# Attention output kept for two blocks: out-projection, norms and FFN spread over all eight units of the next block, tokens held in two tiles

## The chip, the core and the metric

The kernel runs on one core of a Trainium2 chip. The metric is the device time of one execution in microseconds; lower is better. All values are fp32; the queries and keys are split into a rounded part and a remainder (type fp32r) for the score matmuls.

## What is computed

Two sequences of 2048 tokens, 1024 channels, pass through one transformer block. 32 query heads of 32 channels share one key head and one value head.

```python
# x (2, 2048, 1024); wq, wo (1024, 1024); wk, wv (1024, 32); A (8, 16, 1024); B (8, 1024, 16); Wr (8, 1024)
n = layernorm(x)
q, k, v = (n @ wq).reshape(2, 2048, 32, 32), n @ wk, n @ wv
scores = einsum('bqhd,bkd->bhqk', q, k) / sqrt(32)
scores = where(causal, scores, -inf)
attn = einsum('bhqk,bkd->bqhd', softmax(scores), v).reshape(2, 2048, 1024) @ wo
x = x + layernorm(attn)
n = layernorm(x)
gate = 8 * softmax(n @ Wr.T + br)
low = einsum('bsd,hrd->bshr', n, A)
ffn = 2.0 * einsum('bshr,hor,bsh->bso', low, B, gate)
out = x + layernorm(ffn)
```

## The kernel before

Tokens are cut into 8 blocks of 512 (blocks 0 to 3 are the first sequence, 4 to 7 the second) and each block into 4 tiles of 128 tokens. A block's attention runs in 8 units, one for each group of 4 heads, so there are 64 units, called block.unit here: 3.0 is unit 0 of block 3. In a unit the keys are walked in steps of 128. A block sees the keys of its own sequence up to itself, so a unit has 4, 8, 12 or 16 steps in blocks 0, 1, 2, 3 and again in 4 to 7. A step is 4 slots, one for each head; a unit has 16, 32, 48 or 64 slots.

In one slot TensorE computes one score tile (keys by 512 queries, line 1460) and, half a unit ahead, about one tile for the row maxima (line 1449) that VectorE reduces (lines 1059, 1062). ScalarE takes the exponential into one of three buffers `pr` (line 829). Once a step TensorE multiplies the exponentials with the values (line 1488). The softmax denominators are sums over all steps: GpSimd adds the exponentials of a step onto `ds`, 128x2048 elements an add (the first of a unit is line 730, the others 733), and zeroes the masked corner of the last four steps (line 740). For the steps in `by_pe` TensorE sums instead (line 1501): steps 12 to 15, or 10 to 15 in units 6 and 7, where a unit has 16 steps; steps 8 to 11 where it has 12. At the next unit's slot 2 or 6 TensorE reduces `ds` over partitions (line 1523), VectorE takes the reciprocal and scales the unit's output into `ao` (lines 1081, 1086), a ring of `NAO` = 12 buffers. An exponential of step t waits for the add of step t-3, since it writes the same `pr` buffer. GpSimd's first add of a unit waits for the reduction of the previous one, and for the exponentials of step 1.

All other work is placed between these slots by `pieces`: `at(when, engine, stage, ...)` puts a stage at `when`, counted in 64ths of a unit from the block's start, whatever the number of slots; each engine then runs its own list in order.

- `project` (stage "q", line 1414): the query projection of the unit three units later, 8 matmuls with `xT`, from 64th 21 of each unit (46 in unit 5), all in the one PSUM bank `PX`; other places where a unit has 16 slots (`Q0`).
- `post` of the block before: for tile i two halves of the output projection (stage "proj", line 1591, 8 matmuls each, bank `PX`) at 64i+64 and 64i+107, the statistics of the norm on VectorE (`att`), the residual on GpSimd (lines 748, 750), the middle norm, the FFN with its router (`lora`, lines 1623, 1631, 1645) at 64i+154, and the end of the tile on GpSimd (line 759) and SP (store). With 16 slots a unit, where the block before is a long one, the numbers are others.
- `enter` of the next block: the four token tiles are loaded into `t4` in unit 0, VectorE takes their statistics (line 983) in units 0 to 3, GpSimd normalizes them (line 754) in units 1 to 4, TensorE transposes them (line 1539) from the start of unit 5 into `xT`, and the keys and values follow (line 1550).

SP issues all loads and stores in one order too: `residual`, `tokens`, the query stacks (line 625), the rows of maxima (line 631). The block after the last has no slots, so block 7 goes through a tail of its own.

## Time and profile before

| | us |
|---|---|
| median of 3 runs (3362.97 to 3367.23) | 3364.37 |
| the profiled execution | 3359.56 |
| its span, first to last instruction | 3357.8 |

| engine | busy us | share of the span |
|---|---|---|
| TensorE, matmuls | 3199.9 | 95% |
| VectorE | 2277.2 | 68% |
| GpSimd | 2061.7 | 61% |
| ScalarE | 1605.6 | 48% |

| unit of block | 0 | 1 | 2 | 3 | 4 | 5 | 6 | 7 |
|---|---|---|---|---|---|---|---|---|
| block 1, us | 37.9 | 45.5 | 49.8 | 49.7 | 49.8 | 53.6 | 35.3 | 38.8 |
| block 2, us | 48.9 | 57.1 | 62.0 | 62.0 | 61.9 | 63.2 | 49.8 | 53.1 |
| block 3, us | 66.3 | 70.4 | 75.0 | 75.1 | 75.0 | 77.9 | 58.3 | 57.1 |

The busy shares are averages over units with different limits, and matmuls overlap in their pipeline, so 95% isn't TensorE at its peak. The third table reads the span by units: a unit begins where its first score matmul starts. Blocks 5 and 6 differ from 1 and 2 by at most 0.7 us a unit but for unit 5.0, which takes 33.9 us.

### The profile page before, as it was taken

The page shows a single profiled execution, that of the slowest core. Times are in us where ns is not written, and L with a number is a line of the kernel's source. Part 1 is how long each engine was busy: PE and PEld are TensorE (multiplying, and loading weights), DVE is VectorE, ACT ScalarE, POOL GpSimd, SP SyncE. Part 2 cuts the span into 40 slices and gives each one's busy share as a digit, 9 for nine tenths or more (in the row PEclk, how much of TensorE's full clock was granted, in tenths as well). Part 3 has the DMA queues.
Part 4 walks back from the last instruction along what each step waited for, and adds up shares of the span by engine and source line. Part 5 has one row for each costly group of instructions (what it writes and reads, how often), then busy time and mean ns, then how long its engine had stood idle before and what let it go on. Part 6 is the DMA issues. An engine that isn't in the chain of part 4 may idle for free.

```text
span 3357.8 us, 45475 instructions
## 1 busy us (share of the span) xinstructions
PE 3199.9 (95%) x15976; PEld 1608.5 (48%) x15976; DVE 2277.2 (68%) x5974; ACT 1605.6 (48%) x3180; POOL 2061.7 (61%) x741
## 2 busy tenths in 40 slices
PE   7899999999999999999999999999999999999997
PEld 3444454455554455544444445444555444554444
DVE  4776777777778677774366667677777776777605
ACT  2334454455555455555333344445555554555552
POOL 1335676776676888777311176677667577778870
PEclk9999999999999999999999999999999999999998
DMA  4422111110101001001211211112010100011000
GB/s 118 113 61 64 51 51 38 50 38 29 51 23 57 23 23 29 29 23 38 64 51 51 80 45 37 43 39 64 23 57 23 39 17 23 23 38 54 8 1 25
DMA packets 133011, 144.03 MB, mean 43 GB/s; under 512 B 28200, under 2 KB 93736, under 8 KB 132784
## 3 DMA queue, kind: packets, MB, share of 16 engines
q1 hardware_dynamic: 132480, 140.72, 14.3%
q8 instruction: 127, 2.08, 0.3%
q14 instruction: 100, 0.82, 0.1%
q10 hardware_dynamic: 304, 0.41, 0.0%
HBM read 72.91 MB, written 16.78 MB: 27 GB/s over the span
## 4 chain that ended last, share of the span: by engine, by line
PE 74%; POOL 10%; DVE 8%; issue 3%; ACT 2%; SPq 1%; DMA 1%; POOLq 0%; ACTq 0%; DVEq 0%
PE ps L1460 14%; PE ps L1488 13%; PE ps L1449 12%; PE ps L1591 11%; PE ps L1414 11%; POOL ds L733 8%; PE ps L1501 3%; DVE mx L1062 2%; PE ps L1550 2%; POOL ds L730 2%; DVE ps L1081 2%; PE ps L1631 2%; PE ps L1645 1%; SPq L625 1%; PE ps L1523 1%
## 5 line engine op out<-in xcount | busy, mean ns | idle before, releaser
L829 ACT ACTIVATE pr<-ps 128x512 f32<-128x512 f32 (+3 forms) x2560 | 1296.4, 533 | 1387.3 <-PE ps L1460 974.8
L733 POOL TENSOR_TENSOR ds<-ds,pr 128x2048 f32<-128x2048 f32 (+1 forms) x360 | 1492.0, 4145 | 140.3 <-ACT pr L829 108.4
L1460 PE MATMUL ps<-qs,ks 98*128 98x512 f32 (+3 forms) x2560 | 1351.5, 535 | 37.8 <-DVE mx L1062 14.3
L1062 DVE TENSOR_REDUCE mx<-ps 128x1 f32<-128x512 f32 x1536 | 1004.2, 681 | 356.9 <-PE ps L1449 349.2
L1449 PE MATMUL ps<-ks,qs 96*128 96x512 f32 (+3 forms) x2560 | 958.8, 386 | 53.1 <-ACT pr L829 23.3
L1460 PEld LDWEIGHTS ps<-qs,ks 98*128 98x128 f32 x2560 | 483.1, 190 | 784.8 <-issue 313.6
L1059 DVE CUSTOM_DVE_ANT_0 ps<-ps,mask_qk 128x128 f32<-128x128 f32 (+3 forms) x1024 | 491.0, 496 | 428.4 <-PE ps L1449 424.9
L1449 PEld LDWEIGHTS ps<-ks,qs 96*128 96x128 f32 x2560 | 487.8, 193 | 313.0 <-ACT pr L829 145.8
L1488 PE MATMUL ps<-pr,vs 128*32 128x512 f32 (+3 forms) x5120 | 612.1, 546 | 0.6 <-POOL pr L740 0.5
L1414 PE MATMUL ps<-xT,wq_sb 128*128 128x512 f32 x1024 | 513.2, 598 | 5.6 <-ACT zs L856 3.1
L1591 PE MATMUL ps<-wo_sb,ao 128*128 128x512 f32 x896 | 453.5, 598 | 0.5 <-DVE q L1051 0.5
L740 POOL TENSOR_SCALAR_AFFINE_SELECT pr<-pr 128x512 f32<-128x512 f32 x192 | 122.3, 637 | 483.2 <-ACT pr L829 483.2
L730 POOL TENSOR_TENSOR ds<-pr 128x2048 f32<-128x2048 f32 (+1 forms) x56 | 246.2, 4397 | 221.3 <-ACT pr L829 221.3
L1081 DVE RECIPROCAL ps<-ps 128x128 f32<-128x128 f32 x256 | 244.1, 955 | 102.8 <-PE ps L1523 102.7
L1414 PEld LDWEIGHTS ps<-xT,wq_sb 128*128 128x128 f32 x1024 | 186.0, 192 | 83.0 <-issue 59.9
L1488 PEld LDWEIGHTS ps<-pr,vs 128*32 128x32 f32 x5120 | 102.9, 108 | 188.3 <-issue 158.1
L1591 PEld LDWEIGHTS ps<-wo_sb,ao 128*128 128x128 f32 x896 | 164.3, 191 | 57.8 <-issue 35.8
L1059 DVE DVE_READ_ACCUMULATOR2_ANT mx<- 128x1 f32 x1024 | 145.2, 142 | 0.0
L759 POOL TENSOR_TENSOR xr<-xr,zs 128x1024 f32<-128x1024 f32 x28 | 66.5, 2376 | 126.7 <-ACT zs L889 126.7
L1501 PE MATMUL ps<-pr,ones 128*32 128x512 f32 (+3 forms) x1344 | 128.6, 452 | 0.9 <-DVE ao L1086 0.9
L748 POOL TENSOR_SCALAR zs<-zs,r_att 128x1024 f32<-128x1024 f32 x28 | 31.3, 1119 | 138.0 <-DVE r_att L1016 138.0
L1051 DVE TENSOR_TENSOR q<-ps,q 128x512 fp32r<-128x512 f32 x64 | 44.2, 691 | 64.5 <-ACT q L813 64.5
(162 smaller groups left out, 1944.1 us busy)
## 6 DMA issues: line engine op xcount, KB each, us to landing
qs<-q SPq DMA_DIRECT2D x762, 64.0 KB, 2.0
wq_sb<-in_L_attn_wq_dram SPq DMA_DIRECT2D x64, 512.0 KB, 4.0
t<-in_L_attn_x_dram SPq DMA_DIRECT2D x32, 512.0 KB, 6.6
xr<-in_L_attn_x_dram SPq DMA_DIRECT2D x28, 512.0 KB, 4.5
out_dram<-xr SPq DMA_DIRECT2D x28, 512.0 KB, 4.8
wo_sb<-in_L_attn_wo_dram SPq DMA_DIRECT2D x8, 512.0 KB, 5.2
qs<-mT SPq DMA_DIRECT2D x252, 4.0 KB
xT<-in_L_attn_x_dram SPq DMA_DIRECT2D x4, 512.0 KB, 5.8
```

The lines of the kernel that those rows point to most:

```text
L730: nc.gpsimd.tensor_tensor(ds[:, :, c0:], first[:, :, c0:], this, ALU.add).then_inc(added, 1)
L733: nc.gpsimd.tensor_tensor(ds[:, :, c0:], ds[:, :, c0:], this, ALU.add).then_inc(added, 1)
L829: nc.scalar.activation(pr[:, k % NS, g, c0:], ps[:, PM + EXP_PLACE[head(n, t, g)] % NPM, c0:], ACT.Exp, scale=SCALE).then_inc(exp_done, 1)
L1059: nc.vector.tensor_tensor_reduce(out=seen, in0=seen, in1=mask_qk[:, BLK - w:], op0=ALU.add, op1=ALU.max, scale=1.0, scalar=3.0 * NEG, accu ...
L1062: nc.vector.tensor_reduce(found, seen, AX.X, ALU.max).then_inc(mx_done, 1)
L1081: nc.vector.reciprocal(part, part).then_inc(rden_ready, 1)
L1414: last = nc.tensor.matmul(ps[:, PX, :], wq_sb[:, n % NW, k, :], xT[:, k, :], start=(k == 0), stop=(k == KT - 1))
L1449: nc.tensor.matmul(ps[:, bank, 0:w], qs[0:STK, n % NS, g, qt * P:(qt + 1) * P], ks[0:STK, c:c + w], start=True, stop=True).then_inc(mx_rea ...
L1460: last = nc.tensor.matmul(ps[:, bank, c0:], ks[0:STK + 2, c:c + P], qs[0:STK + 2, n % NS, g, c0:], start=True, stop=not by_mask)
L1488: last = nc.tensor.matmul(ps[g * HD:(g + 1) * HD, PPV, c0:], vs[:, row, :], pr[:, (UNIT_STEP[n] + t) % NS, g, c0:], start=(t == 0), stop=( ...
L1501: last = nc.tensor.matmul(ps[g * HD:(g + 1) * HD, PAUX, c0:], ones[:, :], pr[:, (UNIT_STEP[n] + t) % NS, g, c0:], start=(t == by_pe(n)[0]) ...
L1591: last = nc.tensor.matmul(ps[:, PX, :], ao[:, (n + k) % NAO, j % TB * P:(j % TB + 1) * P], wo_sb[:, k, h * HALF:(h + 1) * HALF], start=(k ...
```

## The change

`NAO` grows from 12 to 16, so that `ao` holds two blocks' outputs. `plan_of` gives for each tile five places: first half, second half, load of the residual, middle norm, FFN. For blocks followed by one with 16 slots a unit, and for block 7, they are the old ones. For the blocks 1, 2, 3, 5 and 6 they come from `HALF_AT`: tile 0 has its halves in units 0 and 1, tile 1 both in unit 2, tile 2 in units 3 and 4, tile 3 both in unit 6; the FFN parts stand in units 2, 3, 5 and 7. The query projection moves to the start of every unit but 5 there (in block 7 it stays at 21). The transposes of tiles 0 and 1 move into unit 4, those of tiles 2 and 3 stay in unit 5.

The room for `ao` comes from `t4`, which has two tiles instead of four. Tokens of tiles 0 and 1 are loaded for their statistics, then tiles 2 and 3 into the same room for theirs, then tiles 0 and 1 again for the norm on GpSimd and the transposes, then 2 and 3 again for a norm that now runs on ScalarE. Block 0's tiles 2 and 3 use `xr`, and the tail uses the query-weight buffer for its tiles 2 and 3.

```diff
-    NAO = 12
+    NAO = 16
...
-            Q0, apart = Q_OF[u], Q_LAST if u == 5 else SPREAD
+            Q0, apart = (21 if blk == LAST and u < 5 else Q_OF[u]), Q_LAST if u == 5 else SPREAD
...
+    def plan_of(blk, N):
+
+        if N == 16:
+            return [(t0 + 52, t0 + 92, t0 + 72, t0 + 125, t0 + 128) for t0 in range(0, 256, 64)], 3
+        if blk == LAST:
+            return [(t0 + 64, t0 + 107, t0 + 84, t0 + 149, t0 + 128 + 26) for t0 in range(0, 256, 64)], SPREAD
+        return [(a0, a1, a1 - 10, a1 + 40, a1 + 48) for a0, a1 in HALF_AT], SPREAD
+
+    HALF_AT = ((43, 106), (150, 172), (234, 298), (404, 426))
...
-    Q_OF = (21, 21, 21, 21, 21, 46, 21, 21)
+    Q_OF = (0, 0, 0, 0, 0, 46, 0, 0)
...
-    TURN_AT = (64 * 5, 3)
+    TURN_AT = (64 * 4 + 44, 3)
+    BACK = (20, 14)
...
-        left = t0 + up1 + 15 + later if N == 16 else max(t0 + up1 + 15 + later, (t0 // 64 + 1) * 64 + LEAVE_AT)
+        left = t0 + up1 + 15 + later if N == 16 else min(509, max(t0 + up1 + 15 + later, (t0 // 64 + 1) * 64 + LEAVE_AT))
...
+        back = BACK[N == 16]
+        for i in range(2):
+            at(28 if blk == 1 else 4, "SP", "tokens", blk, i, False)
         for i in range(TB):
             t0 = 64 + 48 * i if blk == 1 else 64 * i + 42
+            at(t0 + 8, "SP", "tokens", blk, (i + 2) % TB, i >= 2)
...
-            at(64 * 4 + 4 + 8 * i if N == 16 else 64 * i + 64 + NORM_AT, "POOL", "norm", blk, i)
+            if i < 2:
+                at(64 * 4 + 4 + 8 * i if N == 16 else 64 * i + 64 * 3 + NORM_AT, "POOL", "norm", blk, i)
+            else:
+                at(T0 + apart * (2 * i - 2) - 1, "SP", "tokens", blk, i, True)
+                for h in range(2):
+                    at(T0 + back + apart * (2 * i + h) - 4, "ACT", "norm", blk, i, h)
...
-        t4 = sb("t4", [P, TB, D])
+        t4 = sb("t4", [P, 2, D])
...
+                if blk and again and i >= 2:
+                    sp.wait_ge(xt_ready, 2 * (TB * blk + i - 2) + 2)
+                elif blk and (again or i >= 2):
+                    sp.wait_ge(LN["pre"]["s_st"], 2 * (TB * blk + (i + 2) % TB) + 2)
+                elif blk:
+                    sp.wait_ge(xt_ready, 2 * (TB * (blk - 1) + i + 2) + 2)
+                sp.dma_start(tokens(blk, i), x_t[blk * TB + i]).then_inc(x_loaded[i], 16)
```

TensorE at the start of unit 3.0, before; 1460 and 1449 are the score and maximum matmuls, 1488 and 1501 the values and sums of unit 2.7, 1523 its reduction.

```order
L1501 MATMUL ps<-pr,ones 32x256 x4
L1460 MATMUL ps<-qs,ks 128x512
L1449 MATMUL ps<-ks,qs 128x512
L1460 MATMUL ps<-qs,ks 128x512
L1449 MATMUL ps<-ks,qs 128x512
L1460 MATMUL ps<-qs,ks 128x512
L1449 MATMUL ps<-ks,qs 128x512
L1488 MATMUL ps<-pr,vs 32x128 x4
L1501 MATMUL ps<-pr,ones 32x128 x4
L1523 MATMUL ps<-ds,ones 32x512 x4
L1460 MATMUL ps<-qs,ks 128x512
```

The same place now; the lines have moved: 1515 and 1504 are the score and maximum matmuls, 1539 and 1552 values and sums, 1574 the reduction, 1469 the query projection.

```order
L1552 MATMUL ps<-pr,ones 32x256 x4
L1515 MATMUL ps<-qs,ks 128x512
L1504 MATMUL ps<-ks,qs 128x512
L1469 MATMUL ps<-xT,wq_sb 128x512
L1515 MATMUL ps<-qs,ks 128x512
L1504 MATMUL ps<-ks,qs 128x512
L1515 MATMUL ps<-qs,ks 128x512
L1504 MATMUL ps<-ks,qs 128x512
L1539 MATMUL ps<-pr,vs 32x128 x4
L1552 MATMUL ps<-pr,ones 32x128 x4
L1515 MATMUL ps<-qs,ks 128x512
L1504 MATMUL ps<-ks,qs 128x512
```

Projection matmuls now stand between the first slots of the unit, ahead of the reduction.

GpSimd in unit 1.7, before: the unit's adds (730 the first, 733 the others) with its masks (740).

```order
L733 TENSOR_TENSOR ds<-ds,pr 128x4x128
L730 TENSOR_TENSOR ds<-pr 128x2048
L733 TENSOR_TENSOR ds<-ds,pr 128x2048
L740 AFFINE_SELECT pr<-pr 128x4x128
L733 TENSOR_TENSOR ds<-ds,pr 128x2048
L740 AFFINE_SELECT pr<-pr 128x4x128
L733 TENSOR_TENSOR ds<-ds,pr 128x2048
L740 AFFINE_SELECT pr<-pr 128x4x128
L733 TENSOR_TENSOR ds<-ds,pr 128x4x384
L740 AFFINE_SELECT pr<-pr 128x4x128
L733 TENSOR_TENSOR ds<-ds,pr 128x4x256
```

The same unit now: 773 and 776 are the adds, 783 the masks, 791 and 793 the residual of tile 3, 803 the end of the tile.

```order
L791 TENSOR_SCALAR zs<-zs,r_att 128x1024
L793 TENSOR_TENSOR xr<-xr,zs 128x1024
L773 TENSOR_TENSOR ds<-pr 128x2048
L776 TENSOR_TENSOR ds<-ds,pr 128x2048
L783 AFFINE_SELECT pr<-pr 128x4x128
L776 TENSOR_TENSOR ds<-ds,pr 128x2048
L783 AFFINE_SELECT pr<-pr 128x4x128
L776 TENSOR_TENSOR ds<-ds,pr 128x2048
L783 AFFINE_SELECT pr<-pr 128x4x128
L776 TENSOR_TENSOR ds<-ds,pr 128x4x384
L803 TENSOR_TENSOR xr<-xr,zs 128x1024
L783 AFFINE_SELECT pr<-pr 128x4x128
```

The residual stands ahead of the first add, and the end of tile 3 ahead of the last mask.

## Rows read from the trace of the kernel before

**Rows 1.** The page, part 4: the chain that ended last, by engine.
```profile
PE 74%; POOL 10%; DVE 8%; issue 3%; ACT 2%; SPq 1%; DMA 1%; POOLq 0%; ACTq 0%; DVEq 0%
```

**Rows 2.** Stretches, one unit each: length, busy us (instructions) by engine, clock, DMA, GB/s.
```profile
core 0: us, PE busy (x) PEld busy (x) DVE busy (x) ACT busy (x) POOL busy (x), PEclk, DMA share, GB/s
256.80:294.70 37.90, 34.15 (x157) 16.03 (x156) 27.23 (x73) 16.97 (x37) 23.40 (x9) 0.92 0.29 92
294.70:340.20 45.50, 45.26 (x192) 22.16 (x188) 27.59 (x72) 18.51 (x37) 29.98 (x13) 0.96 0.14 41
340.20:390.00 49.80, 48.28 (x222) 24.67 (x218) 36.54 (x113) 24.06 (x47) 32.33 (x14) 1.00 0.14 38
...
543.10:578.40 35.30, 33.77 (x168) 16.67 (x164) 28.08 (x67) 16.81 (x35) 28.32 (x12) 1.00 0.19 54
578.40:617.20 38.80, 36.39 (x177) 18.10 (x173) 32.51 (x75) 17.23 (x35) 27.69 (x12) 1.00 0.13 35
...
617.20:666.10 48.90, 46.19 (x248) 22.09 (x244) 36.31 (x87) 25.63 (x51) 40.49 (x16) 1.00 0.22 71
666.10:723.20 57.10, 57.10 (x288) 28.75 (x284) 38.73 (x89) 27.53 (x53) 35.28 (x12) 1.00 0.11 33
723.20:785.20 62.00, 62.00 (x317) 32.06 (x313) 46.78 (x129) 32.88 (x63) 39.07 (x15) 1.00 0.11 31
...
972.30:1022.10 49.80, 48.66 (x264) 24.04 (x260) 38.47 (x84) 26.07 (x51) 36.84 (x13) 1.00 0.14 39
1022.10:1075.20 53.10, 51.41 (x273) 25.17 (x269) 42.85 (x91) 26.46 (x51) 34.38 (x11) 1.00 0.10 26
...
1075.20:1141.50 66.30, 61.46 (x321) 29.18 (x317) 45.99 (x102) 34.04 (x67) 52.85 (x16) 0.95 0.16 51
1141.50:1211.90 70.40, 70.16 (x352) 34.96 (x348) 48.43 (x105) 35.76 (x69) 53.61 (x17) 1.00 0.09 27
1211.90:1286.90 75.00, 74.76 (x381) 38.47 (x377) 56.76 (x145) 41.07 (x79) 57.23 (x19) 1.00 0.09 26
...
1514.90:1573.20 58.30, 55.37 (x313) 25.30 (x309) 27.55 (x76) 33.21 (x67) 45.68 (x14) 1.00 0.11 33
1573.20:1630.30 57.10, 52.46 (x289) 22.11 (x285) 13.97 (x42) 32.19 (x67) 43.57 (x14) 1.00 0.09 24
...
1914.00:1947.90 33.90, 30.77 (x157) 15.39 (x157) 25.73 (x69) 16.56 (x35) 21.37 (x8) 0.99 0.31 102
```

**Rows 3.** Chain that ended last, in time: start us, us, what.
```profile
14.37 5.88 PE ps L1539 x32
...
1656.40 5.15 PE ps L1591 x12
```

**Rows 4.** Timeline of GpSimd in unit 3.0: start, us, what [idle before].
```profile
1082.60 4.56 POOL L730 TENSOR_TENSOR ds<-pr 128x2048 f32<-128x2048 f32 x1 [8.11 <-ACT pr L829]
...
1130.09 4.54 POOL L733 TENSOR_TENSOR ds<-ds,pr 128x2048 f32<-128x2048 f32 x1
```

**Rows 5.** Timeline of GpSimd, the first adds of units 3.1 and 3.2.
```profile
1151.69 4.56 POOL L730 TENSOR_TENSOR ds<-pr 128x2048 f32<-128x2048 f32 x1 [9.25 <-ACT pr L829]
...
1223.19 4.56 POOL L730 TENSOR_TENSOR ds<-pr 128x2048 f32<-128x2048 f32 x1
```

**Rows 6.** Timeline of GpSimd in unit 3.7, its nine adds.
```profile
1579.39 4.56 POOL L730 TENSOR_TENSOR ds<-pr 128x2048 f32<-128x2048 f32 x1 [6.04 <-ACT pr L829]
1584.09 37.43 POOL L733 TENSOR_TENSOR ds<-ds,pr 128x2048 f32<-128x2048 f32 x8
```

**Rows 7.** Timeline of GpSimd in units 2.0 and 2.1: first and seventh add, first add.
```profile
626.00 4.55 POOL L730 TENSOR_TENSOR ds<-pr 128x2048 f32<-128x2048 f32 x1 [2.72 <-ACT pr L829]
...
655.86 4.57 POOL L733 TENSOR_TENSOR ds<-ds,pr 128x2048 f32<-128x2048 f32 x1
...
676.86 4.56 POOL L730 TENSOR_TENSOR ds<-pr 128x2048 f32<-128x2048 f32 x1 [9.77 <-ACT pr L829]
```

**Rows 8.** DMA issues: queue, count, KB each, median us to landing.
```profile
t<-in_L_attn_x_dram SPq DMA_DIRECT2D x32, 512.0 KB, 6.6
```

**Rows 9.** Stretch at the end of unit 3.0, columns as in rows 2.
```profile
1131.00:1135.00 4.00, 4.00 (x18) 0.69 (x17) 1.38 (x2) 0.49 (x1) 4.00 (x2) 0.50 0.00 0
```

More of the change, by code:

```diff
@@ L211, in post @@
     def post(at, blk, N):
[L213 to L217 removed]
+        plan, apart = plan_of(blk + 1, N)
+        for i, (a0, a1, loaded, turned, looked) in enumerate(plan):
+            j = blk * TB + i
+            at(loaded, "SP", "residual", j)
+            for h, first in ((0, a0), (1, a1)):
                 for k in range(KT):
@@ L244, in bass_mqa_sandwich_lora_router, with looked_in, looked_by @@
     IN_RING = ("tr", "turn", "up", "vt")
+    def looked_in(j):
+        n = (j // TB + 1) * NU
+        return n + plan_of(n // NU, slots(n))[0][j % TB][4] // 64
+    def looked_by(n):
+        return sum(looked_in((n // NU - 1) * TB + i) <= n for i in range(TB))
     def beside(j):
```

89 lines of the change are left out of this document (48 added, 41 removed).

## Prediction

> A unit below is one group of four heads; "unit 3.0" is unit 0 of block 3. "Half" is half an output projection of one token tile: 8 matmuls, 16 records in the trace.
>
> **What bounds the kernel now.** I read the page first, then the busy time of each unit's stretch, then GpSimd's own timeline inside the units that are too long. On the page the chain that ended last lies on TensorE for 74% of the span, on GpSimd for 10% and on VectorE for 8% [rows 1]. So it is a kernel bound by TensorE with places where something else leads. The stretches say where. In block 3 unit 0, with no half in it, takes 66.3 us; unit 1, with two halves more, takes 70.4; unit 2, which adds the FFN, 75.0 [rows 2]. One half costs 6.9 us: twelve records run in 5.15 us, so sixteen in 6.87 [rows 3]. Unit 1 less two halves is 56.6 us, so unit 0 holds 9.7 us in which TensorE waits. The same subtraction gives 43.3 for block 2, against 48.9 in unit 2.0 (5.6 of waiting), and 31.7 for block 1, against 37.9 in unit 1.0 (6.2). Unit 5.0 with 33.9 waits for only 2.2 [rows 2].
>
> GpSimd explains unit 3.0: its adds start 7.4 us into the unit (1082.60 less 1075.2) and run without a gap until 1134.63, 52.0 us for eleven; 6.9 us later the unit ends [rows 4]. An exponential needs the buffer that the add three steps earlier reads, so from there GpSimd's pace, 4.7 us for each four slots, sets the time. Unit 3.1 has its first add at 10.2 us (1151.69 less 1141.5) [rows 5], because eight projection matmuls stand in its first 18 slots: 10.2 + 52.0 + 6.9 = 69.1, close to its 70.4. It is thus nearly at GpSimd's floor too, although it looks like TensorE's work.
>
> **The change, part by part.** Every block 1, 2, 3, 5 and 6 carries eight halves, four FFN parts, the next block's transposes and its eight query projections before and after. TensorE's work doesn't change; only waits can be won or lost, and so I take each unit's new length as the larger of its work and its floor. The halves per unit go from 0,2,2,2,2,0,0,0 to 1,1,2,1,1,0,2,0; the FFN parts from units 2 to 5 to units 2, 3, 5 and 7; half of the transposes from unit 5 to unit 4 (16 of 32; the head's 32 took 5.88 us [rows 3], so up to 2.9, and as some of them stand beside other waits I take 1.9 to 2.4). The query projection goes from slot 21 to slot 0 of all units but 5. An FFN part is 62.0 less 57.1, 4.9 us in block 2, 4.3 in block 1, 4.6 in block 3 [rows 2].
>
> Block 3. Units 0 and 1 hold 56.6 + 6.9 = 63.5 us of work, but the projection at slot 0 moves the first add to 10.2: 10.2 + 52.0 + 6.9, and 0.7 for the matmuls of the half that stand behind the last add, 69.8 each (+3.5, -0.6). Unit 2 stays. Unit 3: work 68.1; GpSimd has the residual ahead of its first add, which then starts at 11.3 (1223.19 less 1211.9) [rows 5]: 70.6 (-4.4). Unit 4: 69.9 (-5.1). Unit 5: -1.9. Unit 6: 58.3 and two halves, less the waits that they fill; it has 24 maximum matmuls fewer than unit 0 and 16 row-sum records more (313 records against 321 [rows 2]), so I estimate its work at 53 and the waits at 5.3: 66.8 (+8.5). Unit 7 has nothing of the post-processing before; its first add is at 6.2 (1579.39 less 1573.2), nine adds end 42.1 later at 1621.5, and 8.8 remain [rows 6]. Now the query projection and the residual of tile 3 stand ahead: 11.3 + 42.1 + 8.8 = 62.2 (+5.1). Sum for block 3: +5.1 us. It loses.
>
> Block 2, and 6 like it. GpSimd's floor: first add at 10.8 (676.86 less 666.1), then 34.4 to the end of its seventh add and 5.7 to the unit's end, from unit 2.0 (626.00 there to 660.43, end 666.1) [rows 7]: 50.9, with the last matmuls of a half 52.3. Units 0 and 1: 52.3 (+3.4, -4.8). Unit 3: work 55.1, 55.3 with a little waiting (-6.7). Unit 4: 53.2 (-8.8). Unit 5: -2.0. Unit 6: 49.8 + 13.8, less 3.6 of filled waits (its work by the same count some 45, of which VectorE's order keeps one), 60.0 (+10.2). Unit 7: +4.9, the price of its FFN part, with nothing hidden: VectorE is busy 42.85 us of its 53.1 already, and the FFN and middle norm bring 8.0 (46.78 less 38.73) [rows 2]. Sum: -3.8 us each.
>
> Block 1. GpSimd has only seven adds, four of them narrow, and no floor appears. Units 0 and 1: 38.6 of work, 39.0 (+1.1, -6.5). Unit 3: 43.2 (-6.6), unit 4: 41.5 (-8.3), unit 5: -2.4, unit 6: 35.3 + 13.8 - 0.7 = 48.4 (+13.1), unit 7: 38.8 + 4.3 + 1.3 = 44.4 (+5.6), the 1.3 because VectorE has 8.95 us more to do (36.54 less 27.59) and 6.3 free [rows 2]. Sum: -4.0. Block 5 is the same but for its unit 0, 33.9 before, 39.0 now (+5.1 instead of +1.1): 0.0.
>
> Blocks 0 and 4 (16 slots a unit) only get the new loads. Tiles 2 and 3 are fetched again once the first two tiles are transposed, and ScalarE, no longer GpSimd, normalizes them, at slots 1 to 3 of unit 5. Four loads in a row land after a median of 6.6 us [rows 8]; the first is issued some four slots, a quarter of a unit, ahead of its use: 8 us where a unit takes what 5.0 does, less in block 0. ScalarE waits with its exponentials behind it, and TensorE's transposes behind them: between 0 and 4 us, and I take 2.0 for block 0 and 1.0 for block 4. The Trainium skill, DMA: Bandwidth & Descriptors, section Anatomy of one DMA, prices a transfer as 2.0 us and bytes over 436 GB/s, an estimate of 3.2 us for such a tile; by that ScalarE would not wait in either block, and the sum were 2 to 3 us lower. The row is of four transfers sharing the queue, two share it now; it counts for more. The earlier loads of tiles 2 and 3 stand behind VectorE's statistics on SP's queue; the rows of maxima behind them have slack, so nothing is counted.
>
> Block 7 keeps its plan. It inherits one thing: tile 3 leaves on GpSimd at slot 61 of unit 7 of the block before, ahead of the last mask. An add of that size is 2.4 us; most lies beside the tail of the unit, and I count 0.5. Sixteen buffers of attention output mean no new wait, since the projections that read a buffer end in unit 6 and it is written again two units later. The tail's scratch in the weight buffer waits for a projection long over: nothing.
>
> Sum: 2.0 - 4.0 - 3.8 + 5.1 + 1.0 + 0.0 - 3.8 + 0.5 = -3.0 us. The profiled execution has 3359.56 us, 1.8 more than its span; the median of the runs is 3364.37. So 3361.4 by the median, 3362 rounded.
>
> **TensorE's clock.** At the end of unit 3.0, after TensorE had waited for GpSimd, the granted clock is 0.50 over 1131 to 1135, the lower level (1.2 GHz) [rows 9]. The half that now stands there fills that wait, so I expect the stretch to go from its place; with the floor set by GpSimd it gives nothing back, which is why no term of the sum has it. But slots 18 to 42 of units 3.0, 3.1 and 3.4 now hold only scores beside GpSimd's pace, and the drop may come there. The Trainium skill, TensorE: Matmul & The Clock Gate, Part 1, says that activity releases the throttle and idleness brings it back. By that rule the new thin stretch is as exposed as the old one was; the second rival below prices it from the rows.
>
> **Rivals.** (a) The waits of units 5, 6 and 7 are filled by the work moved beside them instead of persisting. VectorE's load in unit 1.7 is 32.5 + 8.9 = 41.4 against my 44.4, in unit 2.7 42.9 + 8.0 = 50.9 against 58.0. Unit 1.7 then gives 3 us and unit 2.7 four to seven, and each unit 5 two of its waits: about 5 us in blocks 1 and 5 each, 7 in 2 and 6, 4 in block 3: 28 us less, 3334. For it: a wait of one engine beside work of another is the usual place to win. Against it: VectorE works in order, and 6.3 us free in unit 1.7 is spread over all of it.
> (b) Slower: GpSimd's pace leaves TensorE thin between slots 18 and 42, and the granted clock halves there. A stretch like that of [rows 9] is at least 4 us at half speed and delays TensorE by 2. In the nine units with a floor and one half (0, 1 and 4 of blocks 2, 3 and 6) that is 18 us: 3380. It decides when TensorE can't catch up before slot 42. Against it: unit 3.7, thin throughout, shows 1.00 before [rows 2].
> (c) Slower: the second load of tiles 2 and 3 is late. If ScalarE waits 4 us in blocks 0 and 4 and 1.5 in the five others, that is 12 us more than counted: 3374.
>
> **How the numbers follow.** A difference of under 0.2% (6.7 us) can't be told from none, so 3357.7 to 3371.1 is "the same". Chances: the sum 0.48 (it may slip by some 8 us: 0.15 faster, 0.28 same, 0.05 slower), (a) 0.27, (b) 0.18, (c) 0.07. Faster 0.41, same 0.29, slower 0.30. The range reaches to (a) and (b) with their slips: 3330 to 3384.
>
> **What would show it.** Units 3.0 and 3.1 at 69 to 71 us with GpSimd's adds gapless from 10.2 us on; block 3 longer by 3 to 7 us, blocks 2 and 6 shorter by 2 to 6; unit 2.7 at 56 to 60; unit 0.5 longer by about 2. I am wrong if unit 3.0 stays at 66 (then the projection ahead costs nothing), if GpSimd shows gaps, or if unit 2.7 is under 54.

## The result and the profile after

| | before | after |
|---|---|---|
| time, median | 3365.69 us (3362.97 to 3367.23) | 3382.49 us (3381.87 to 3383.68) |
| ratio | | 1.0051, interval 1.0034 to 1.0069 |
| span of the profiled execution | 3357.8 us | 3381.9 us |
| mean granted clock of TensorE | 0.985 | 0.977 |

The changed kernel is slower by 0.5%, where 0.07% faster was forecast. The medians differ by 16.8 us, the two profiled spans by 24.1: the profiled execution of the kernel before (3359.56 us) is shorter than all four of its timed ones, that of the changed kernel (3383.68) is the longest of its four. What follows unit by unit compares these two executions, so its sum overstates the difference by some 7 us.

Page of the changed kernel, parts 1 (busy us, share of the span, instructions) and 4 (the chain that ended last, by engine), and one line of part 6 (DMA issues: queue, count, KB each, median us to landing):

```profile
PE 3216.4 (95%) x15976; PEld 1616.4 (48%) x15976; DVE 2274.6 (67%) x5974; ACT 1616.5 (48%) x3208; POOL 2045.4 (60%) x727
...
PE 73%; POOL 10%; DVE 8%; issue 3%; ACT 3%; SPq 2%; DMA 1%; POOLq 0%; ACTq 0%; DVEq 0%
...
t<-in_L_attn_x_dram SPq DMA_DIRECT2D x58, 512.0 KB, 3.4
```

The chain hardly differs from [rows 1]: averages over the whole span say nothing on this change. TensorE has as many instructions as before. The 58 token loads, 26 more than before, land in a median of 3.4 us, not in 6.6 as in [rows 8].

The stretches of the changed kernel, one unit each (1.3, 1.4, 1.6, 1.7, 2.3, 2.7, 3.0); columns as in [rows 2]:

```profile
390.30:438.30 48.00, 44.18 (x205) 22.22 (x201) 34.95 (x109) 22.11 (x45) 34.22 (x15) 0.93 0.17 51
438.30:478.30 40.00, 39.28 (x192) 19.52 (x188) 25.90 (x65) 19.54 (x41) 31.27 (x14) 1.00 0.28 86
...
530.10:576.20 46.10, 45.76 (x201) 22.51 (x197) 29.36 (x68) 18.44 (x37) 30.30 (x13) 1.00 0.18 52
576.20:625.90 49.70, 45.29 (x205) 22.90 (x201) 42.41 (x117) 22.09 (x45) 32.40 (x14) 0.90 0.10 28
792.90:849.60 56.70, 56.08 (x302) 29.04 (x298) 44.51 (x127) 31.38 (x62) 40.87 (x15) 1.00 0.14 43
1024.10:1083.90 59.80, 57.50 (x302) 29.48 (x298) 51.71 (x132) 31.50 (x61) 39.82 (x14) 0.97 0.08 22
1083.90:1153.30 69.40, 65.53 (x336) 31.62 (x332) 46.82 (x103) 34.01 (x68) 53.08 (x16) 1.00 0.16 50
```

Unit 1.3 of the kernel before, for comparison:

```profile
390.00:439.70 49.70, 48.13 (x221) 24.59 (x217) 36.49 (x113) 24.05 (x47) 34.65 (x15) 1.00 0.16 49
```

The ends of a window are rounded to 0.1 us, so a length below can differ by 0.1 from its line. 1.3 lost a half (221 records to 205, 6.9 us of TensorE's work) and became 1.8 us shorter. 1.4 lost a half and its FFN and became 9.7 shorter (49.8 to 40.0). 1.7 got an FFN, forecast at 5.6 us, and became 11.0 longer (38.8 to 49.8), with VectorE busy 42.41 of 49.70 us. In both units with an FFN TensorE is idle for about 4 us, and the granted clock is 0.93 and 0.90.

Sums by block, change in us against the kernel before (forecast beside it):

| block | 0 | 1 | 2 | 3 | 4 | 5 | 6 | 7 | sum |
|---|---|---|---|---|---|---|---|---|---|
| forecast | +2.0 | -4.0 | -3.8 | +5.1 | +1.0 | 0.0 | -3.8 | +0.5 | -3.0 |
| measured | +4.9 | +3.9 | 0.0 | +2.2 | +6.6 | +4.7 | +0.1 | +1.7 | +24.1 |

Of the 27.1 us between the two sums blocks 1 and 5 carry 12.6, blocks 0 and 4 8.5, blocks 2 and 6 7.7, block 7 1.2, and block 3 gives 2.9 back.

GpSimd in units 3.0 and 3.7 of the changed kernel (start us, us, instruction, idle before), the answer to [rows 4] and [rows 6]:

```profile
1094.13 4.56 POOL L773 TENSOR_TENSOR ds<-pr 128x2048 f32<-128x2048 f32 x1 [9.82 <-ACT pr L873]
1098.91 42.28 POOL L776 TENSOR_TENSOR ds<-ds,pr 128x2048 f32<-128x2048 f32 x9 [0.22 <-ACT pr L873]
...
1588.40 4.57 POOL L773 TENSOR_TENSOR ds<-pr 128x2048 f32<-128x2048 f32 x1 [1.03 <-ACT pr L873]
1593.12 37.50 POOL L776 TENSOR_TENSOR ds<-ds,pr 128x2048 f32<-128x2048 f32 x8
```

The first add of 3.0 starts 10.2 us into the unit, as forecast, and no gap over 0.6 us stands between the eleven.

### The profile page after: what moved, and what is told of

It reads as the page before. It is cut to its first block, busy times and chain, and to the rows that moved or that the text cites. A ratio compares the mean times of both kernels' runs of the same rounds, so it can differ in the third digit from the quotient of the medians.

```text
span 3381.9 us, 45564 instructions
## 1 busy us (share of the span) xinstructions
PE 3216.4 (95%) x15976; PEld 1616.4 (48%) x15976; DVE 2274.6 (67%) x5974; ACT 1616.5 (48%) x3208; POOL 2045.4 (60%) x727
## 4 chain that ended last, share of the span: by engine, by line
PE 73%; POOL 10%; DVE 8%; issue 3%; ACT 3%; SPq 2%; DMA 1%; POOLq 0%; ACTq 0%; DVEq 0%
PE ps L1515 14%; PE ps L1539 13%; PE ps L1504 12%; PE ps L1469 11%; PE ps L1645 10%; POOL ds L776 9%; PE ps L1552 3%; DVE mx L1117 2%; PE ps L1604 2%; SPq L666 2%; PE ps L1699 1%; PE ps L1685 1%; PE ps L1574 1%; PE ps L1655 1%; DVE ps L1136 1%
## 5 line engine op out<-in xcount | busy, mean ns | idle before, releaser
L1504 PE MATMUL ps<-ks,qs 96*128 96x512 f32 (+3 forms) x2560 | 965.9, 390 | 49.8 <-ACT pr L873 19.4
L1539 PE MATMUL ps<-pr,vs 128*32 128x512 f32 (+3 forms) x5120 | 619.6, 554 | 0.7 <-POOL pr L783 0.5
L1106 DVE TENSOR_TENSOR q<-ps,q 128x512 fp32r<-128x512 f32 x64 | 44.2, 691 | 62.0 <-ACT q L857 61.9
```

The source lines that it names most:

```text
L1504: nc.tensor.matmul(ps[:, bank, 0:w], qs[0:STK, n % NS, g, qt * P:(qt + 1) * P], ks[0:STK, c:c + w], start=True, stop=True).then_inc(mx_rea ...
L1539: last = nc.tensor.matmul(ps[g * HD:(g + 1) * HD, PPV, c0:], vs[:, row, :], pr[:, (UNIT_STEP[n] + t) % NS, g, c0:], start=(t == 0), stop=( ...
```

## The experiments

Each is one profiled execution read unit by unit, with timed rounds where a ratio is given. In several of them the edit doesn't touch blocks 0 and 4, and these still differ: with one and the same code in block 0, profiles of the changed kernel and its variants have 205.7 to 221.0 us for it, and its unit 0.6 alone 25.1 to 30.0. So a difference of up to 5 us in one of the units 0.0, 0.2, 0.5, 0.6, 0.7, 4.0, 4.6 and 4.7 is no evidence. Most units of 32 slots and more repeat within 0.3 us where nothing near them changed, but some have two lengths 1.5 to 1.7 us apart, and there the granted clock differs. Units x.y of blocks 1 and 5, and of 2 and 6, have the same instruction lists. 1.2 and 5.2 of the changed kernel, and 2.7 and 6.7 of e5 (a variant below):

```profile
338.10:390.30 52.20, 49.59 (x222) 25.31 (x218) 37.03 (x116) 23.63 (x47) 31.66 (x15) 0.97 0.16 46
2005.80:2056.30 50.50, 47.88 (x221) 24.58 (x217) 36.91 (x116) 23.60 (x47) 31.63 (x15) 1.00 0.16 48
...
1028.40:1088.20 59.80, 57.48 (x301) 29.72 (x297) 51.65 (x132) 31.62 (x61) 39.77 (x14) 0.97 0.08 22
2704.20:2762.50 58.30, 55.97 (x302) 28.88 (x298) 51.61 (x132) 31.45 (x61) 39.85 (x14) 1.00 0.09 22
```

In each pair the longer unit has 3.4 us at half clock and the other none; TensorE's busy time is longer by 1.7 and 1.5 us and the unit by about as much. But 5.3 and 5.7 of the changed kernel, the partners of 1.3 and 1.7:

```profile
2056.30:2104.10 47.80, 43.67 (x205) 21.92 (x201) 34.95 (x109) 22.13 (x45) 34.27 (x15) 0.96 0.17 51
2242.00:2291.70 49.70, 46.19 (x205) 23.76 (x201) 42.44 (x117) 22.09 (x45) 32.38 (x14) 0.87 0.10 27
```

5.7 has 3.4 us more at half clock than 1.7 (13.1 against 9.6) and takes the same 49.7 us; 1.3 has 3.4 us more than 5.3 (6.8 against 3.4) and takes 0.2 us longer. So a half-clock stretch costs nearly its lost full-speed time (half its length) in some units and next to nothing in others, and the second kind, 1.3, 1.7, 5.3 and 5.7, are the units that e12 below shows to be held by VectorE. It isn't a strict rule: 5.3 of e7, with the same instructions and 6.8 us at half clock, took 49.3.

### e1: the query projection back at slot 21

```
-    Q_OF = (0, 0, 0, 0, 0, 46, 0, 0)
+    Q_OF = (21, 21, 0, 21, 21, 46, 0, 21)
```

> The kernel after, with the query projection back at 64th 21 of units 0, 1, 3, 4 and 7 (it stays at 0 in units 2 and 6, whose halves need the place). Theory A: in the 32-slot blocks TensorE reaches the FFN's transposes (slots 13 and 14) before the norm's chain (GpSimd residual, VectorE, ScalarE) has delivered, because the projection that stood at slots 10 to 19 is gone; and in blocks 3, 2 and 6 the projection at slot 0 delays GpSimd's first add. Then units 1.3 and 5.3 fall from 48 to about 44, units 1.7 and 5.7 from 49.7 to about 46, units 3.0 and 3.1 from 69.3 to about 67.5, and the sum is 20 to 28 us less than the kernel after: about 3358. Rival B: VectorE's own work bounds unit 1.7 and the waits in 1.3 are its order: then 1.7 and 1.3 stay within 1 us and only block 3's units move, 5 us in all: about 3377.

Measured: 3412.56 us, ratio 1.0146 (1.0123 to 1.0169), 30 us above the changed kernel. Theory A is out: 1.3 rose to 51.7, and rival B is out for it too. Block 3 alone won, 5.3 us under before, since 3.0 and 3.1 fell to 66.5 and 66.2: GpSimd's floor begins with the projection ahead of its first add, as the forecast had it. But 1.7 rose to 51.6, 2.3 to 60.5 and 2.7 to 64.2. The projection at slot 21 stands beside the FFN of these units; that this is why they rose wasn't tested by itself.

### e2: the new token loads with the old places of halves and FFN

```
-        if blk == LAST:
+        if blk:
...
-    Q_OF = (0, 0, 0, 0, 0, 46, 0, 0)
+    Q_OF = (21, 21, 21, 21, 21, 46, 21, 21)
```

> The tokens' part alone: two tiles, second loads, norms of tiles 2 and 3 on ScalarE, transposes at their new places, 16 buffers of attention output; halves, FFN and query projection at the old places in every block. Theory A: blocks 0 and 4 show the same growth as in the kernel after (+5 and +6 us), all because of this part, and the other blocks stay within 2 us of before: 12 to 14 us over before, about 3378. Rival C: this part costs 2 to 3 us as forecast, and the growth in blocks 0 and 4 comes with the moved halves (what they leave behind at a block's end): about 3368.

Measured: 3371.69 us, ratio 1.0031 (1.0016 to 1.0045). So the loads, norms and transposes have a cost of their own, 8 of the changed kernel's 17 us over before by the medians, and the halves, FFNs and projections carry the rest; the two intervals overlap, so the split is rough. Blocks 0 and 4 grow by 4.0 and 5.1 (4.9 and 6.6 in the changed kernel), blocks 2 and 3 by 2.1 and 2.7. Units 0.5 and 4.5 show it in every variant: +4.1 and +3.7 here.

### e3: the kernel before with one half moved

```
-            for h, first in ((0, t0 + a0), (1, t0 + a1)):
+            for h, first in ((0, 43 if i == 0 and N > 16 else t0 + a0), (1, t0 + a1)):
```

> The kernel before with one edit: the first half of tile 0's output projection stands at 64th 43 of unit 0 instead of 0 of unit 1, in the blocks with 32 slots and more. Nothing else moves, 12 buffers suffice. By the floors of the prediction (a half fills the wait at the end of unit 0, and GpSimd's first add in unit 1 comes earlier, since nothing stands at its start): blocks 1 and 5 save 5 to 6 us, 2 and 6 4 to 5, 3 and 7 about 1 each: 16 to 22 us less than before, about 3347. If a half in unit 0 costs its 6.9 us there and unit 1 gives only as much back, nothing changes: 3365.

Measured: 3351.47 us, ratio 0.9965 (0.9952 to 0.9977), 12 us under before. Only tile 0's first half goes to unit 0. Its stretches of 1.0 and 1.1:

```profile
259.50:298.20 38.70, 37.44 (x174) 18.36 (x173) 27.95 (x73) 17.92 (x38) 24.63 (x9) 1.00 0.28 89
298.20:335.80 37.60, 37.12 (x177) 18.36 (x173) 26.92 (x72) 17.51 (x36) 28.80 (x12) 1.00 0.18 50
```

Unit 1.0 had 3.8 us of idle TensorE and a clock of 0.92 [rows 2]: with a half more it is 0.7 us longer, and 1.1 is 7.9 shorter. Blocks 1 and 5 gain 7.6 and 4.0 us, what the change got from its units 0 and 1, without its price. In blocks 2 and 6, where 4 to 5 us each were expected, nothing was gained (+0.6 and -0.9): 2.0 rose by 4.3 as 2.1 fell by 5.2.

### e4: FFN of tiles 0 to 2 eight positions later

```
-        return [(a0, a1, a1 - 10, a1 + 40, a1 + 48) for a0, a1 in HALF_AT], SPREAD
+        return [(a0, a1, a1 - 10, a1 + 40, a1 + (48 if a0 > 400 else 56)) for a0, a1 in HALF_AT], SPREAD
```

> The kernel after with the FFN part of tiles 0, 1 and 2 8/64 of a unit later behind their middle norm (4 slots in the 32-slot blocks), tile 3 unchanged. Theory A: the wait at the FFN's transposes goes: units 1.3 and 5.3 fall from 48 to 45 or 46, units 1.2 and 5.2 from 52.2 and 50.5 to 50, unit 1.5 by about 1, the rest stays: about 3375. Rival B (VectorE's load and order): nothing moves by more than 1 us, about 3382.

Measured: 3386.91 us, ratio 1.007 (1.0043 to 1.0097). 1.3 went from 48.0 to 47.4, 5.3 up by 0.7, 1.2 and 5.2 by 0.1 and 0.2: the distance of the FFN from the middle norm isn't the cause.

### e5: GpSimd's residual addition ahead of its other work

The changed kernel has a wait that the one before has not (engine, line, waited for: us in total, times, longest):

```profile
DVE st_mid L1038 <- POOL xr L793: 13.6, 8, 2.7
```

VectorE's middle-norm statistics stand in slots 11 to 13 of 1.3 with the maxima behind them; the residual they need comes after GpSimd's token norm and the last addition of the tile before.

```
-    NORM_AT = 1
-    LEAVE_AT = 1
+    NORM_AT = 12
+    LEAVE_AT = 12
```

> The changed kernel with GpSimd's token norm and its last addition of a tile (output to DRAM) moved from the first slots of a unit to 12 of its 64 positions later, so that in units 1.2, 1.3, 1.5 (and those of block 5) the residual addition of the next tile is GpSimd's first such work. Theory A: the changed kernel loses in 1.3 and its like because VectorE's middle-norm statistics wait 1.2 to 2.7 us for that addition (13.6 us in 8 waits) and the maxima behind them come late. Then the waits fall to under 2 us in all, 1.3 goes from 48.0 to 44.5..46.5, 5.3 alike, 1.2, 1.5, 5.2 and 5.5 lose 0.5 to 1.5 us each, and the whole is 6 to 12 us under the changed kernel: 3371 to 3377. Theory B: the waits stand beside time that TensorE's own load and its clock fill anyway; then the waits go but 1.3 stays within 1 us of 48.0 and the whole within 3 us of 3382.5.

Measured: 3399.28 us, ratio 1.0101 (1.0072 to 1.013). In 1.3 and 5.3 the wait went (2.7 us to nothing) and the units fell by 0.7 and 0.6 only, so Theory A, which I held after reading the two traces, is out for them. In 1.2 and 1.5 the waits (1.2 and 2.7 us) stayed: GpSimd had nothing ahead of the residual there. (1.2 fell to 50.5 all the same, with none of its 3.4 us at half clock.) Meanwhile 2.3 and 6.3 rose by 5.8, 3.3 and 3.4 by 3.3 and 3.2: the two instructions now stand between GpSimd's adds, and these units are at its floor. ScalarE at slot 12 of 1.3 in this kernel, and TensorE beside it:

```profile
407.91 0.82 ACT L918 ACTIVATE zs<-xr,mm,r_mid 128x512 f32<-128x512 f32 x1 [3.12 <-DVE mm L1228]
...
407.86 0.49 PE L1515 MATMUL ps<-qs,ks 98*128 98x512 f32 x1 [2.14 <-DVE mx L1114]
```

Both wait for VectorE, which does this in the meantime, without a pause:

```profile
405.78 0.68 DVE L1106 TENSOR_TENSOR q<-ps,q 128x512 fp32r<-128x512 f32 x1
406.38 0.95 DVE L1136 RECIPROCAL ps<-ps 128x128 f32<-128x128 f32 x1
407.24 0.50 DVE L1114 CUSTOM_DVE_ANT_0 ps<-ps,mask_qk 128x384 f32<-128x384 f32 x1
407.66 0.14 DVE L1114 DVE_READ_ACCUMULATOR2_ANT mx<- 128x1 f32 x1
407.66 0.21 DVE L1228 TENSOR_SCALAR mm<-mv_mid,r_mid 128x1 f32<-128x1 f32 x1
```

This is where the next theory comes from: the query's addition (moved here by the projection at slot 0), the four reciprocals of 0.95 us and the middle norm's chain stand in the same slots.

### e6: transposes of tiles 2 and 3 two slots later in units 0.5 and 4.5

```
-    BACK = (20, 14)
+    BACK = (20, 22)
```

> The changed kernel with the transposes of tiles 2 and 3 (and the token norms ahead of them) 8 of 64 positions, two slots, later in the two-copies part of blocks 0 and 4: units 0.5 and 4.5. Theory A: 0.5 (+4.1 us over before) and 4.5 (+3.7) are long because in their first four slots eight transposes and the last tile's FFN wait for each other through ScalarE, which also does the token norms. Then with the two apart 4.5 goes from 41.9 to 39..40.5 and 0.5 falls by 0 to 2 us: 3378 to 3382. Theory B: it is the bare amount of work in 4.5 (16 transposes and four ScalarE norms more than before); then 4.5 stays at 41.5..42.5, or grows by 1 to 3 us as the key projection that needs these transposes comes late: 3382 to 3386. Whatever it does, 4.7 keeps its 33.2 us if that is set by the clock and not by the order in 4.5.

Measured: 3390.33 us, ratio 1.0074 (1.0045 to 1.0103). 4.5 rose from 41.9 to 44.2, with 10.2 us at half clock for 6.8, and 4.6 and 4.7 took 61.5 us for 60.6: the growth of 4.5 that Theory B has. Moved later the transposes and norms cost more, and not less; that the key projection waits for them is argued from the order and not shown.

### e7: tile 3's halves 20 positions earlier

```
-    HALF_AT = ((43, 106), (150, 172), (234, 298), (404, 426))
+    HALF_AT = ((43, 106), (150, 172), (234, 298), (384, 406))
...
-    Q_OF = (0, 0, 0, 0, 0, 46, 0, 0)
+    Q_OF = (0, 0, 0, 0, 0, 46, 43, 0)
```

```
-        return [(a0, a1, a1 - 10, a1 + 40, a1 + 48) for a0, a1 in HALF_AT], SPREAD
+        return [(a0, a1, a1 - 10, a1 + 40, max(a1 + 48, 468 * (a0 > 320))) for a0, a1 in HALF_AT], SPREAD
```

> The changed kernel with the last tile's two half projections 20 of 64 positions earlier in units x.6, the query projection of x.6 behind them, and its middle norm so in the end of x.6 and not in x.7; its FFN begins 6 positions earlier. Theory A: x.7 costs 11 us more than before in block 1 (where I forecast 5.6) because in its slots 9 to 13 the chain of the middle norm, the four reciprocals and the query's copy and addition meet on VectorE and ScalarE. Then 1.7 goes from 49.8 to 44..46.5, 5.7 alike, 2.7 and 6.7 from 59.8 by -1..-4, and x.6 grows by 0 to 2 us: in all -6 to -14, 3368 to 3376. Theory B: it is the FFN's load on TensorE and VectorE, wherever the middle norm stands; then 1.7 stays at 49..50.5 and the whole within 4 us of 3382.5.

Measured: 3383.63 us, ratio 1.0059 (1.0036 to 1.0082). 1.7 fell by 2.1 and 1.6 rose by 2.0 (2.7 by -2.1, 2.6 by +3.5). Some two microseconds go where the halves and the middle norm go; the other nine of 1.7's growth stay with the FFN.

### e8: more work for TensorE in a thin unit

Here the question is what the granted clock costs. Units 4.6 and 4.7 in the kernel before, then in the changed one, which has the same instructions there:

```profile
1856.50:1883.80 27.30, 23.83 (x140) 12.06 (x140) 20.68 (x47) 8.41 (x21) 0.00 (x0) 1.00 0.19 50
1883.80:1914.00 30.20, 27.89 (x148) 14.54 (x148) 22.67 (x59) 8.35 (x19) 0.00 (x0) 0.89 0.17 45
```

```profile
1870.90:1898.30 27.40, 23.87 (x141) 12.10 (x141) 20.77 (x47) 8.37 (x21) 0.00 (x0) 1.00 0.19 49
1898.30:1931.50 33.20, 32.00 (x149) 16.46 (x149) 22.68 (x59) 8.35 (x19) 0.00 (x0) 0.74 0.15 40
```

4.6 is the same in both, with TensorE idle 3.5 us of 27.4, and then 4.7 runs at half clock (1.2 GHz) for 6.8 us in one and 17.1 in the other; some 148 records keep TensorE busy 27.89 or 32.00 us. The edit puts six matmuls into 4.6:

```
+        if N == 16 and blk and u == 6:
+            for when in (20, 24, 28, 32, 56, 60):
+                at(64 * u + when, "PE", "warm", n + 3 + (when > 40))
...
+            def warm(n):
+                bank_left("q", n)
+                nc.tensor.matmul(ps[:, PX, :], wo_sb[:, 0, 0:P], wo_sb[:, 0, 0:HALF], start=True, stop=True)
```

> The changed kernel with six additional matmuls of 128x512 (operands from the out-projection's weights, result overwritten by the next query projection, so the output doesn't change) in the thin slots of unit 4.6 alone: four in its slots 5 to 8, two in 14 and 15. Nothing of unit 4.7 is changed. Theory C: the changed kernel is slower where the granted clock falls after thin stretches; 4.7 takes 33.2 us against 30.2 with the same instructions because its half-clock stretch is 17.1 us long and not 6.8. With TensorE busier in 4.6 the fall at the start of 4.7 is gone or short: 4.7 is 26.5 to 30.5 us, 4.6 grows by 0.5 to 2.5 us (27.4 to 28..30), block 4 falls by 0.5 to 5 us and the whole is 3377 to 3382. Theory B (the clock's falls are idle time's shadow and cost nothing of their own): 4.7 stays within 0.7 us of 33.2 whatever its granted clock is, and the whole grows by what 4.6 does, 3383 to 3385.

```profile
1874.90:1903.30 28.40, 28.00 (x152) 14.06 (x152) 20.43 (x46) 8.33 (x21) 0.00 (x0) 1.00 0.18 48
1903.30:1935.10 31.80, 29.14 (x150) 14.12 (x148) 22.74 (x60) 8.15 (x19) 0.00 (x0) 0.89 0.16 42
```

Measured: 3382.77 us, ratio 1.0048 (1.0031 to 1.0065), no change. 4.7 fell to 31.8 with a clock of 0.89, 4.6 rose by 1.1. That is between the theories, but it doesn't show that the six matmuls did it: e7, e12 and e13, which have block 4's code of the changed kernel, also have 6.8 us at half clock in 4.7, and take 30.4 us for it, behind a 4.6 of 27.3. Here is 4.7 in e7:

```profile
1901.50:1931.90 30.40, 28.04 (x148) 14.63 (x148) 22.55 (x59) 8.35 (x19) 0.00 (x0) 0.89 0.17 44
```

So with the same instructions 10.3 us more at half clock, 5.1 us of lost full-speed time, go with 2.8 us of length. The clock has a price of its own. In 4.7 it is about half of the lost full-speed time, in 1.2 and 2.7 nearly all of it, in 1.7 nothing.

### e9: middle norm and FFN of tiles 0 and 1 ten positions later

```
-        return [(a0, a1, a1 - 10, a1 + 40, a1 + 48) for a0, a1 in HALF_AT], SPREAD
+        return [(a0, a1, a1 - 10, a1 + (50 if a1 < 200 else 40), a1 + (58 if a1 < 200 else 48)) for a0, a1 in HALF_AT], SPREAD
```

> The changed kernel with the middle norm and the FFN of tiles 0 and 1 ten of 64 positions later (units x.2 and x.3), behind the reciprocals that stand in slots 7 to 10 of a unit of two-key-block length, and behind the query's addition in slot 9. Theory D: 1.3 keeps 48.0 us although a half projection left it, because in its slots 9 to 13 these all meet on VectorE, ScalarE waits 3.7 us for the middle norm's mm with the exponentials behind it, and TensorE idles 3.8 us (1.6 before). Then with the norm later that wait falls under 1.5 us, 1.3 takes 44.5..46.5 us, 5.3 alike, 2.3 and 6.3 change by -2..+0.5, 1.2 by -2..+1, in all -4 to -10: 3373 to 3379. Theory B: the FFN's own work on VectorE (some 10 us a tile) bounds such a unit wherever the chain stands; then 1.3 and 5.3 stay at 47.3..48.7 and the whole within 3 us of 3382.5.

Measured: 3400.2 us, ratio 1.0103 (1.0082 to 1.0123). 1.3 rose to 49.2, 5.3 to 49.6, 2.3 to 60.0, 3.3 to 75.8, while 1.2 fell to 49.2 (block 1 in all +0.3). Theory D is out: away from the reciprocals the chain isn't cheaper, it only comes later.

### e10: e3 and the six matmuls of e8

> The kernel before with tile 0's first half projection in unit 0 (e3) and the six additional matmuls in unit 4.6. In e3 block 4, of which nothing was changed, took 4.6 us more than before, in 4.6 (+3.1) and 4.7 (+1.0), each beside a half-clock stretch of 6.8 us. Theory C: with TensorE busy there, 4.6 takes 28..30 us and 4.7 26.5..30.5, the sum 55..59 against 61.6 in e3 and 57.5 before: the whole 3345 to 3351. Theory B: 4.6 takes as long as in e3 or 1 to 2 us longer, 4.7 31.2, the whole 3351 to 3355.

The edit is that of e3 and that of e8. Measured: 3349.37 us, ratio 0.9951 (0.9937 to 0.9966). 4.6 and 4.7 together 60.8 against 61.6 in e3. The two medians, 3349.4 and 3351.5, can't be told apart.

### e11 and e12: which engine bounds a unit with an FFN

Both are single executions and leave work out in units x.3 and x.7 of blocks 1, 2, 5 and 6: e11 six of eight steps of the query projection (TensorE, twelve records), e12 most columns of the reciprocals (VectorE).

```
+                    if blk and N in (32, 48) and u in (3, 7) and 0 < k < KT - 1:
+                        continue
```

```
+                if n >= NU and slots(n + 1) in (32, 48) and (n + 1) % NU in (3, 7):
+                    part = part[:, 0:8]
                 nc.vector.reciprocal(part, part).then_inc(rden_ready, 1)
```

> The changed kernel with six of the eight matmul steps of the query projection left out in units x.3 and x.7 of blocks 1, 2, 5 and 6 (the queries made there lack three quarters of their sum, so the output is another): some 6 us of TensorE work a unit gone, nothing of VectorE's, ScalarE's or GpSimd's. It asks which engine bounds the units that hold an FFN. Theory P (TensorE's load, as the forecast had it): 1.3 falls from 48.0 to 42..44, 1.7 from 49.8 to 44..46, 2.3 from 56.7 to 51..53, 2.7 from 59.8 to 54..56. Theory V (VectorE's and ScalarE's chains hold the first half of such a unit, so TensorE work taken out of it turns into waiting): 1.3 and 1.7 fall by 0 to 2.5 us each; 2.3 and 2.7, whose slots hold more of TensorE's own work, by 3 to 5.

> The changed kernel with the four reciprocals of units x.3 and x.7 of blocks 1, 2, 5 and 6 on 8 of 128 columns (the output is another): 3.0 to 3.5 us of VectorE work a unit gone, from slots 7 to 10, nothing of TensorE's. Theory V: 1.3 and 1.7 fall by 1.5 to 3.5 us each, 2.3 and 2.7 by 0 to 2. Theory P: no unit falls by more than 0.6 us.

The stretches of 1.3, 1.7 and 2.3 in e11:

```profile
404.30:452.50 48.20, 40.43 (x193) 20.48 (x189) 34.66 (x109) 21.74 (x44) 34.07 (x15) 0.89 0.17 50
590.70:642.20 51.50, 45.38 (x194) 23.03 (x190) 42.33 (x117) 22.39 (x45) 32.16 (x14) 0.82 0.10 27
808.30:864.40 56.10, 53.49 (x289) 27.13 (x285) 44.52 (x127) 31.23 (x62) 40.89 (x15) 0.97 0.15 44
```

and of 1.3, 1.7, 2.3 and 2.7 in e12:

```profile
386.90:430.90 44.00, 41.97 (x205) 21.64 (x201) 32.10 (x109) 22.10 (x45) 34.27 (x15) 1.00 0.19 55
569.10:615.70 46.60, 44.91 (x205) 23.08 (x201) 39.55 (x117) 22.07 (x45) 32.42 (x14) 0.89 0.11 29
782.50:839.30 56.80, 56.18 (x302) 29.10 (x298) 42.52 (x127) 31.37 (x62) 40.91 (x16) 1.00 0.15 43
1013.80:1071.40 57.60, 56.05 (x301) 28.96 (x297) 49.11 (x132) 31.32 (x61) 39.79 (x14) 1.00 0.09 23
```

Twelve records less, some 5 us of TensorE's work, made 1.3 no shorter (48.0 to 48.3), 1.7 longer (49.8 to 51.5) and 5.7 shorter by 0.2. TensorE's idle time in 1.3 doubled, from 3.8 to 7.8 us, and the granted clock went from 0.93 to 0.89 in 1.3 and from 0.90 to 0.82 in 1.7; in 5.7 it stayed at 0.87. With less to do TensorE waited more. 2.85 us less for VectorE (34.95 to 32.10) made 1.3 shorter by 4.0, 5.3 by 3.8, 1.7 and 5.7 by 3.1 each. In 1.3 the clock also rose to 1.00, but in 1.7 it was as before (0.89 for 0.90), so there the 3.1 us come from VectorE's 2.86 alone. This settles which engine bounds these units. 2.7 fell by 2.1, some 1.5 of it the clock's (2.7 has two lengths, 59.8 and 58.3). In e11 2.3 and 2.7 fell by 0.6 and 0.8, not by the 3 to 5 of Theory V, and e12 left 2.3 as it was: GpSimd's pace holds it, as e5 showed from the other side. e12 took 3356.04 us in its one run, 26 less than the changed kernel.

### e13 and e14: the same reciprocals, spread

```
-            first, apart = 3 if by_pe(n - 1) else 6 if N == 16 else 7, 2 if by_pe(n - 1) and N > 16 else 1
+            first, apart = 3 if by_pe(n - 1) else 6 if N == 16 else 7, 2 if N > 16 else 1
```

e13 is the changed kernel with this, e14 is e3 with it.

> The changed kernel with the four reciprocals of a unit of 32 or 48 slots in every second slot (7, 9, 11, 13, the scaling at 15) and not in 7 to 10 with the scaling at 11; no work is added or left out. Taking 3.4 us of reciprocals away shortened 1.3 by 4.0 and 1.7 by 3.1 us, so VectorE bounds there; open is whether it is the heap in slots 7 to 11 or the sum of its work over the unit. Theory H (the heap): 1.3 and 5.3 fall by 1 to 3 us, 1.7 and 5.7 by 1 to 3, the whole is 3370 to 3378. Theory S (the sum): they stay within 0.7 us, and the whole within 3 us of 3382.5.

> The kernel before with tile 0's first half projection in unit 0 (e3) and the reciprocals spread the same way. In its units x.2 to x.4 TensorE's load bounds (49.8 us with two halves and an FFN), so Theory H gives little there, 0 to 1 us a unit in units of 32 slots, and something in 1.6, 1.7, 5.6 and 5.7, which have little TensorE work: 0.5 to 1.5 us each. The whole 3343 to 3351; Theory S: 3350 to 3353.

Measured for e13: 3386.81 us, ratio 1.0067 (1.0043 to 1.0091). 1.3 fell by 1.0, 5.3 by nothing, 1.7 and 5.7 rose by 2.1 and 2.6: mostly Theory S, the sum of VectorE's work over the first half of such a unit.

Measured for e14: 3334.14 us (3328.4 to 3335.13), ratio 0.9905 (0.9887 to 0.9923): 30 us under the kernel before, 48 under the changed one, and better than either theory had it. Its units 1.3, 1.4 and 1.5:

```profile
382.70:431.70 49.00, 48.13 (x222) 24.65 (x218) 36.36 (x113) 23.91 (x47) 34.64 (x15) 1.00 0.17 49
431.70:480.70 49.00, 48.15 (x222) 24.66 (x218) 33.76 (x101) 23.92 (x47) 34.63 (x15) 1.00 0.17 49
480.70:530.50 49.80, 47.08 (x241) 25.20 (x237) 36.75 (x107) 25.86 (x51) 33.43 (x14) 1.00 0.14 38
```

Against e3 1.2, 1.3 and 1.4 are 0.8 shorter each and 1.5 3.4 shorter; block 1 gains 6.3 us and block 5 5.6. Of the 17 us that e14 is under e3, these two blocks hold 12. Why the same spreading helps here and not in e13 wasn't tested; what differs is that these units have two halves for TensorE to run.

### e15: the edit of e12 on the kernel before

> The kernel before with the four reciprocals of units x.3 and x.7 of blocks 1, 2, 5 and 6 on 8 of 128 columns (the output is another): the edit that took 4.0 us from 1.3 and 3.1 from 1.7 of the changed kernel. If 1.3 of the kernel before (49.8 us, two halves, a query projection and an FFN) is bound by TensorE, as the forecast had it, it falls by 0 to 0.7 us here; if it was near VectorE's bound too, by 1.5 to 3. 1.7, with neither halves nor FFN, 0 to 2. The unit that falls tells where VectorE bounded before the change.

Unit 1.3:

```profile
393.50:441.20 47.70, 47.70 (x222) 24.79 (x218) 33.72 (x113) 24.05 (x48) 34.65 (x15) 1.00 0.17 51
```

It fell by 2.2 us to 47.7, all of it busy TensorE; 5.3 fell by 2.1, 1.7 by 0.6. So before the change 1.3 stood 1.6 us of waiting above TensorE's own busy time, and those came from VectorE. A unit 97% busy on TensorE still fell by 2 us when VectorE had less to do.

## Why the prediction was wrong

**The rows it rested on were right, and so was GpSimd's floor.** Forecast for 3.0 and 3.1 69.8 each, measured 69.4 and 69.1; for 3.3 and 3.4 70.6 and 69.9, measured 71.4 and 69.3. First add at 10.2 us, no gaps, no 66 in unit 3.0. Unit 3.7 came out at 61.5 for 62.2 partly by luck: its first add stands at 8.7 us and not 11.3, and 10.5 us follow the last one and not 8.8. Two of the sums carry a slip: 3.3's own terms (11.3, 52.0, 6.9) give 70.2, and the 1.4 us that block 2 has for the last matmuls of a half come from no row. Block 3 lost 2.2 us where 5.1 was forecast.

**The step that failed** is "I take each unit's new length as the larger of its work and its floor", with work meaning TensorE's and GpSimd's floor the only one, but for 1.3 us that VectorE got in 1.7. It fails in the units of 32 slots that have an FFN. Terms, forecast and measured: 1.3 -6.6 and -1.8; 5.3 -6.6 and -2.0; 1.7 and 5.7 +5.6 and +11.0; 1.2 0 and +2.4. The overshoots of these five and 5.2 (+0.8) make 23.4 us of the 27.1, and the other units of blocks 1 and 5 give 10.8 of them back (1.6 was forecast at +13.1 and took +10.8). e11 and e12 show the cause in 1.3, 1.7, 5.3 and 5.7: VectorE bounds them, with the FFN's statistics and roots, the middle norm, the reciprocals and the maxima in one queue. A unit with an FFN takes 48 to 52 us whether it has no half (1.7), one (1.3) or two (1.2); without an FFN it takes 40.0 with one and 46.1 with two. 1.2 and 5.2 weren't tested by leaving work out; 1.6 of the 2.4 us in 1.2 is the clock, which 5.2 shows without. Before the change three of a block's four FFNs stood beside two halves each (the fourth beside transposes and the key projection), where TensorE's work covered VectorE's load but for some 2 us (e15); the change took the cover from 1.3 and put an FFN into 1.7, which had none. The prediction had the number in hand, VectorE's 41.4 of 44.4 us in 1.7, and its argument against rival (a), that VectorE works in order, was the argument for a much longer unit. It used it only to deny a gain.

**Blocks 2 and 6** came out at 0.0 and +0.1 instead of -3.8 each. GpSimd's pace holds 2.0, 2.1 and 2.4 as forecast (adds without a gap over 0.6 us). The terms were close: 2.1 -5.9 for -4.8, 2.3 -5.2 for -6.7, 2.4 -9.2 for -8.8, 2.6 +10.0 for +10.2, 2.7 +6.7 for +4.9, 2.0 +4.3 for +3.4. Of 2.7's excess 1.5 us is the clock: without its 3.4 us at half clock it takes 58.3 (e4, e5, e13), where 58.0 was forecast. That 48 slots of TensorE's work cover most of VectorE's is argued.

**Blocks 0 and 4**: +2.0 and +1.0 forecast for a late load. The load isn't late: it lands in 3.4 us, and ScalarE waits for it once, 0.5 us; rival (c) is out. The Trainium skill, DMA: Bandwidth & Descriptors, section Anatomy of one DMA, gives a formula for transfers issued from GpSimd, 3.2 us for this size, an estimate; these are issued by SP, and their median of 3.4 us is near it, while other loads of the same size in this kernel have medians of 4.0 to 5.7. Taking the 6.6 of [rows 8], four transfers at once, was the wrong choice. What the runs show instead is unit 5: with eight transposes and four half norms more there, 4.5 takes 3.7 us more and 0.5 3 to 5 (32.1 to 34.9 against 29.2 to 30.9 with the code of before). 4.5 also has 6.8 us at half clock in the changed kernel and none before, so how much is work and how much clock stays open; 4.4, which gave transposes away, is 0.8 shorter. The rest of blocks 0 and 4, 4.7's 3.0 us above all, is the granted clock in units that the change doesn't touch, and not steady: kernels with the code of before there (e3, e14, e15) have 61.4 to 61.6 us for 4.6 and 4.7 together, the profile of before 57.5, the changed kernel 60.6.

**The rivals.** (a), the filled waits, is out: 1.7 is 49.8 and not 41.4, 2.7 59.8 and not 51. (b) named the measured time almost (3380 for 3382.5), for a reason that the runs bear out in part only. The granted clock is lower, 0.977 for 0.985, and lost full-speed time (1 less the clock, times the span) is 78 us against 50. But it now fell in 1.3 and 1.7, beside VectorE's work, and in 4.7, whose code is as before, and not in slots 18 to 42 of the nine units where the rival put it: 3.0 is at 1.00 after and 0.95 before, and what 2.0 and 6.0 have (4.0 and 3.9 us at half clock) is the end of a stretch that begins in 1.7 and 5.7. How much of the 24 us is the clock's own can be told in part, from units with the same instructions: 1.6 us in 1.2, 1.5 each in 2.7 and 6.7, 2.8 in 4.7 and 2.4 in 0.0 (29.8 with 10.2 us at half clock, 27.4 with 3.4 in e12), less 2.7 in 0.6, where the kernel before had the half-clock stretch: 7 us, an estimate. In 1.3 and 1.7 a further 3.4 us of it cost next to nothing, as 5.3 and 5.7 show. What it has in 4.5 and the others is open.

**The gain of units 0 and 1** came about as forecast: 1.1 -7.5 and 5.1 -7.0, for +0.6 in 1.0 and +2.5 in 5.0. e3 gets the same from one line.

## What to carry to other kernels

Before pricing a move by one engine's work, write down for each stretch what every engine has to do in it, and treat a moved piece as a load on each: an FFN part with its norm cost 4.3 us beside two half projections and 11 us where no half stood beside it. Look for the piece that can be moved from a stretch where its engine is the bound into one where it is idle, and move only that: one half projection a block gave 12 us, the whole new plan with its loads lost 17. Before a difference of a microsecond or two is put down to an edit, look whether a unit with the same instructions has it too. Where a unit's engine seems full, test it by taking work from another one; leaving out a few microseconds on each in turn tells the bound in two runs.

## What the runs showed of the hardware

- Less work for TensorE needn't mean less time: with 12 records fewer of 205, 1.7 took 51.5 us for 49.7, its clock at 0.82 for 0.90 and its busy time at 45.4 us for 45.3, and 5.7 took 49.5 us for 49.7, its clock at 0.87 both times.
- The same instructions in unit 4.7 took 30.2 to 33.2 us, with 6.8 to 17.1 us at half clock. Kernels with the same code in all of block 4 show both (33.2 in the changed kernel, 30.4 in e7, e12 and e13), so what decides between them isn't known from these runs.
- 3.4 us at half clock lengthened 1.2 by 1.7 us and 2.7 by 1.5, and 1.7 by nothing: the price depends on whether TensorE is what the unit waits for.
- A reciprocal of 128x128 takes 0.955 us on VectorE, a multiplication of 128x512 0.68: per column more than five times as much. The Trainium skill, VectorE: DVE Perf Modes, section Walkthrough: the 8-slice pipeline in each mode, says that a reciprocal is an iterative divide with a repeat count of 8. The longer time per column fits that; no run here shows the mechanism. The four reciprocals of a unit are 3.8 us in the engine that bounds it.
